# Quantised attention stage: values projected behind the queries, bias split and residual moved to other engines, one comparison per threshold, and a new order of every engine's instructions

## Time and profile before

| | before |
|---|---|
| median of 3 runs | 3001.84 us (2989.6 to 3002.13) |
| profiled execution, its own time | 3000.46 us |
| its span | 2998.6 us |
| PE busy | 2708.6 us (90%) |
| DVE busy | 1938.4 us (65%) |
| ACT busy | 1374.7 us (46%) |
| POOL busy | 1243.1 us (41%) |
| mean granted clock of TensorE | 0.934 of full speed |

### The profile page before, as it was taken

How to read it: one execution, slowest core, us unless ns; L and a number is a source line. 1 busy time by engine, 2 the same in 40 slices (tenths; PEclk the granted TensorE clock), 3 DMA queues, 4 the chain that set the end, 5 groups by cost and what they waited for, 6 DMA issues and landing times. The chain is left out here.

```text
span 2998.6 us, 65391 instructions
## 1 busy us (share of the span) xinstructions
PE 2708.6 (90%) x23572; PEld 2325.2 (78%) x23572; DVE 1938.4 (65%) x4184; ACT 1374.7 (46%) x3256; POOL 1243.1 (41%) x1637
## 2 busy tenths in 40 slices
PE   7999999978999999999997999867777888599995
PEld 7999999966888888888887788755666666477774
DVE  5565555556777777777775544357766666466666
ACT  3222222235666666666665333233333333266665
POOL 2111111125767767676774011223333434334434
PEclk9999999998999999999999999977777878799998
DMA  5000000001000000000000100000000000000001
GB/s 179 7 7 7 7 7 7 3 10 51 4 5 3 5 5 3 5 3 5 3 5 24 50 0 0 8 28 8 8 7 7 7 7 0 18 30 28 28 11 57
DMA packets 43501, 49.58 MB, mean 17 GB/s; under 512 B 4064, under 2 KB 33728, under 8 KB 43168
## 3 DMA queue, kind: packets, MB, share of 16 engines
q1 hardware_dynamic: 43424, 48.55, 4.9%
HBM read 35.96 MB, written 4.19 MB: 13 GB/s over the span
## 5 line engine op out<-in xcount | busy, mean ns | idle before, releaser
L587 POOL TENSOR_TENSOR a_probs<-a_probs,a_rs 128x512 f32<-128x512 f32 x64 | 70.7, 1104 | 466.7 <-DVE a_rs L443 466.7
L1108 ACT ACTIVATE b_probs<-bank,b_shift,b_q_scale 128x128 f32<-128x128 f32 x512 | 228.5, 461 | 0.6
L1173 POOL TENSOR_TENSOR b_rows<-b_rows,b_swapped 128x512 f32<-128x512 f32 x160 | 204.6, 1287 | 57.3 <-DVE b_swapped L946 57.3
L1220 POOL TENSOR_TENSOR b_probs<-b_probs,b_rs 128x512 f32<-128x512 f32 x128 | 133.4, 1042 | 137.8 <-DVE b_rs L998 134.7
L531 ACT COPY a_pT<-bank 128x512 f32<-128x512 f32 x64 | 37.6, 587 | 308.7 <-PE bank L324 308.7
L448 DVE TENSOR_TENSOR a_oT<-bank,a_oT 128x512 fp32r<-128x512 f32 x128 | 82.5, 687 | 144.1 <-ACT a_oT L536 144.1
L1183 POOL TENSOR_TENSOR b_rms<-b_rms,sh_minus_half 128x8 f32<-128x8 f32 (+1 forms) x128 | 170.6, 1333 | 10.7
L954 DVE TENSOR_REDUCE b_ss<-b_squares 128x4 f32<-128x512 f32 x192 | 125.3, 681 | 73.5 <-ACT b_squares L1083 73.5
L2728 ACT ACTIVATE d_probs<-d_probs,d_unit_q 128x512 f32<-128x512 f32 x128 | 90.5, 721 | 163.5 <-DVE d_probs L2612 163.0
L46 PE MATMUL bank<-a_xT,early_wq 128*128 128x256 f32 x512 | 150.4, 294 | 13.1 <-DVE early_wq L73 10.5
L46 PE MATMUL bank<-early_wo,b_oT 128*128 128x256 f32 x512 | 150.3, 293 | 1.4 <-DVE b_oT L920 1.4
(11 more groups left out here) (379 smaller groups left out, 9252.8 us busy)
## 6 DMA issues: line engine op xcount, KB each, us to landing
a_xT_in<-in_xT SPq DMA_DIRECT2D x16, 256.0 KB, 2.6
sh_x<-in_x SPq DMA_DIRECT2D x1, 4096.0 KB, 18.7
b_ctx_in<-in_ctxT SPq DMA_DIRECT2D x32, 128.0 KB, 2.0
d_x_in<-sh_x SPq DMA_DIRECT2D x16, 256.0 KB, 2.3
e_x_in<-sh_x SPq DMA_DIRECT2D x16, 256.0 KB, 2.3
e_cT<-in_ctxT SPq DMA_DIRECT2D x32, 128.0 KB, 2.5
out<-sh_x SPq DMA_DIRECT2D x16, 256.0 KB, 2.1
a_qT<-in_L_attn_Wq SPq DMA_DIRECT2D x4, 512.0 KB, 6.3
```

What stands on the lines that cost most here:

```text
L1108: op = act.activation(probs[:, g % 2, keys], bS[:, keys], ACT.Exp, bias=shift[:, g % 2, a:a + 1], scale=q_scale[:, g, a // 2, a % 2:a % 2 ...
L1173: pool.tensor_tensor(rows[:, unit, :], rows[:, unit, :], swapped[:, half, :], ALU.add).then_inc(added[unit], 1)
L1220: pool.tensor_tensor(pr, pr, rs[:, g % 2, :].unsqueeze(2).to_broadcast([128, R, 128]), ALU.mult).then_inc(probs_ready[g], 1)
```

```diff
-            def project_columns(bank, m, o):
+            def project_columns(i, bank, m, o, ready):
...
                 for c in range(C):
-                    exact(out, parts(lambda a: wq[:, m, a, c, o * 128:(o + 1) * 128]), (qx.result[:, c, :], qx.result[:, c, :]), c == 0)
-                return pe.matmul(out, qx.y_both[:, o * 128:(o + 1) * 128], of_chunk[:, m, :], start=False, stop=True)
+                    for a in range(2):
+                        pe.matmul(out, wq[:, m, a, c, columns], qx.result[:, c, :], start=(c == 0 and a == 0), stop=False)
+                pe.matmul(out, qx.y_high[:, columns], of_chunk[:, m, :], start=False, stop=False)
+                pe.matmul(out, qx.y_low[:, columns], of_chunk[:, m, :], start=False, stop=True).then_inc(ready, 1)
...
                 for c in range(C):
-                    op = pe.matmul(bank[0:q.reps, c * 128:(c + 1) * 128], q.cmax[:, c, :, :].rearrange("p k m -> p (k m)"),
-                                   sh.ident[:, :], start=True, stop=True)
+                    for j in range(len(weights)):
+                        pe.matmul(bank[32 * j:32 * j + 32, c * 128:(c + 1) * 128], q.cmax[:, c, :, :].rearrange("p k m -> p (k m)"),
+                                  sh.ident[:, :], start=True, stop=True)
...
-            def both_y(i, q, used):
...
-                dve.scalar_tensor_tensor(q.y_both[:, :], q.y_high[:, :].bitcast(F32), keep_low[0:q.reps, :], q.y_whole[:, :],
-                                         ALU.mult, ALU.add).then_inc(q.y_both_ready, 1)
...
+            def exceed(i, q):
...
+                dve.tensor_tensor(q.exceeds[:, :, :, :], q.cmax[:, :, 0, :].unsqueeze(3).to_broadcast([128, C, M, N_THR]),
+                                  q.thr[:, :, :].unsqueeze(1).to_broadcast([128, C, M, N_THR]), ALU.is_gt).then_inc(q.is_above, 1)
...
-                dve.tensor_tensor(q.by_column(q.clipped[:, :]), q.by_column(q.steps[:, :]), q.of_top(LEAST), ALU.max).then_inc(q.raw_scale, 1)
+                dve.scalar_tensor_tensor(q.by_column(q.clipped[:, :]), q.of_top(INVERSE), 1e-9, q.by_column(q.steps[:, :]),
+                                         ALU.mult, ALU.max).then_inc(q.raw_scale, 1)
+
+            def rescale(i, q):
...
+                dve.tensor_tensor(q.by_column(q.scale[:, :]), q.by_column(q.clipped[:, :]), q.of_top(UNIT), ALU.mult).then_inc(q.scale_ready, 1)
...
-                for r in range(2):
-                    op = dve.scalar_tensor_tensor(sh.res[:, r, :], bX[0][:, r * D:(r + 1) * D], unit_c[:, r:r + 1], xb[:, r, :], ALU.mult, ALU.add)
-                op.then_inc(res_ready, 1)
...
+            def take_y(i, r):
...
+                act.wait_ge(y_ready, this(i))
+                act.wait_ge(qc.unit_rows_ready, this(i))
+                act.wait_ge(res_ready, last(i))
+                op = act.activation(y_scaled[:, r, :], bX[0][:, r * D:(r + 1) * D], ACT.Copy, scale=unit_c[:, r:r + 1])
+                if r == 1:
+                    op.then_inc(scaled, 1)
...
-                pool.wait_ge(q.compared, nth(i.n, 2, 1))
-                hold(pool, sh.passed_pool)
-                pool.tensor_scalar(above, above, 0.0, None, ALU.is_gt).then_inc(q.compared, 1)
...
+            def low_y(i, q, used):
...
+                pool.tensor_tensor(q.y_low[:, :], q.y_whole[:, :], q.y_high[:, :].bitcast(F32), ALU.subtract).then_inc(q.y_low_ready, 1)
...
+            def residual(i):
...
+                pool.wait_ge(scaled, this(i))
+                pool.wait_ge(xb_ready, this(i))
+                pool.wait_ge(norm_done, last(i))
+                hold(pool, sh.passed_pool)
+                pool.tensor_tensor(sh.res[:, :, :], y_scaled[:, :, :], xb[:, :, :], ALU.add).then_inc(res_ready, 1)
```

```diff
+                exponent(new, 0)
+                exponent(new, 1)
+                take_y(old, 0)
+                take_y(old, 1)
+                take_pT(new, 0)
```

415 lines of the change are left out of this document (203 added, 212 removed).

## The result

| | before | with the change |
|---|---|---|
| median of 4 runs each | 3001.32 us (2989.6 to 3002.13) | 2832.16 us (2824.01 to 2835.54) |
| profiled execution, its own time | 3000.46 us | 2824.01 us |
| its span | 2998.6 us | 2822.2 us |
| mean granted clock of TensorE | 0.934 | 0.973 |

The ratio is 0.9441 (0.9409 to 0.9473): 5.6% faster. A difference of 0.3 us between the mean turns of two kernels is therefore not clear of noise; turns that are wholly at full clock agree in both profiles (27.3 to 27.5).

A forecast was written before the change was run, and what follows sets the result against it. It took a chain through one bank, with no engine full, to bound the quantised stage. Fourteen turns falling from 38.8 to 29.5 us give 130, with 12 at fill and drain 142: 3000.5 - 142 = 2858 us, range 2825 to 2915.

The forecast's parts named there:

- four parts (maxima, K, old rows, output): Old quantised turn of 38.8 us: x's chain, old rows' chain, output and residual follow each other through one bank.
- the wait in it for GpSimd: Old rows' divide and restore take 2.35 and 2.26 us during GpSimd's key spread, against 0.69 for x's restore.
- the walk through the new turn: New turn followed from x's turning at full clock: K's copy at 15.1, next x at 28.5, plus 1.0.
- fill and drain: First slots, last two turns and tail around the fourteen full turns: together 12 us less.
- TensorE's floor: Rival: TensorE's 25.2 us of work sets the turn, hand-offs hidden, 26 to 28 a turn, 2809 to 2837 us; chance 0.08.
- hand-offs: End of the new turn: 1.0 us added for waits between engines and one likely half-rate stretch, giving 29.5.
- Contention: Old rows' divide and restore beside GpSimd's key spread: 3.2 us of the chain lost in the turn shown.
- the five: Savings from x's maxima to K's copy: comparison 1.1, y_both 0.5, old maxima earlier 2.0, clock 0.8, multiplication 0.2; 4.6 in all.
- Half rate for two fifths of the time: Rival: TensorE's clock stays at 0.80 in the turns, 34 us a turn, 2921 us; chance 0.22.
- Keys late: Rival: a turn is K's copy plus 13.7; with K's copy at 29.3, 43.0 a turn, 3047 us; chance 0.06.

The follow-up runs named there:

- out of the way: Changed kernel with GpSimd's residual first, both low_y together, VectorE's shift and moments ahead of clip and rescale: 2823.15 us, ratio 0.9415.
- three passes: Changed kernel with GpSimd's three-pass comparison in place of VectorE's comparison and GpSimd's multiplication: 2874.29 us, ratio 0.9585.
- residual on VectorE: Changed kernel with the residual on VectorE again, last in its list, without ScalarE's scaled copies and GpSimd's sum: 2865.01 us, ratio 0.9551.
- fewer matmuls: Changed kernel without the eight matmuls that add the low part of the bias products: 2840.14 us, ratio 0.9473.
- the run: Changed kernel with the copy of K behind the restore of the old rows in VectorE's list: 2956.37 us, ratio 0.9883.

## Why the prediction was right, and where it was off

**What was right.** The chain of the old kernel with its four parts (maxima, K, old rows, output), the wait for GpSimd in it, and the points of the walk through the new turn, within 0.7 us up to the output. A clock above 0.9 was forecast too.

**The sum.** Predicted were turns of 29.5, 12 us at fill and drain, 2858 us. Against the profiled execution the miss is 34 us: 13 x (29.5 - 27.5) = 27 in the turns, 2.4 at the fill (5.4 for 3.0) and 5 behind (23.3 for 18.5). The median lies 8 us above that execution, hence 26. The turn of 27.5 and 2832 us are not in the likeliest band (28 to 31.5, chance 0.61) but in that of the rival *TensorE's floor*, whose words were "the hand-offs are hidden, 26 to 28 a turn, 2809 to 2837", with a chance of 0.08. The range held the result only because it took in half of that rival. The way and the direction were right; that the number came out inside is in part luck.

**The step that was off** is the last of the walk: "27.6 to 28.6, later with the hand-offs between ... I take 28.5 and add 1.0 for hand-offs". The next x was turned at 27.4 in the turn shown. The walk itself held, point by point (predicted, measured from 2081.79): x's maxima 4.1, 4.3; K's copy 15.1, 15.2; keys spread 20.0, 19.7; clip 18.1, 17.9; rescale 20.2, 19.8; old rows restored 23.6 to 24.6, 22.95; output 25.7, 26.3 (the terms given for the output, 20.0 + 2.1 + 0.6 + 1.2 + 1.5, make 25.4). After the restore its words "Then two maxima and two shifts 2.4, the exponent 0.721, two scaled copies of the output 0.9" were wrong: the copies start as the output is done and stand behind no exponent. The wait of "up to 1.0 behind GpSimd's normalisation" did not come (it was GpSimd that waited, see the end), and the half-rate stretch that the +1.0 partly stood for is in two of thirteen turns only. From K's copy to the next x the prediction had 28.5 - 15.1 = 13.4 and 1.0 for hand-offs, and it was 12.1 to 12.2. No row stood for the hand-offs; most of them must lie inside the rows' distances already, so they were counted twice.

**The bound was named wrongly.** "VectorE ... leaves 23. It is then no bound, only its order is." The 23 is what VectorE's work is: 26.4 busy less 3.6 of waiting is 22.8. The prediction had the rescale wait behind the keys in its walk (2.1 us predicted, 1.8 measured) and left it out of VectorE's list; the restore of x behind `low_y` and residual, 1.6 us, it did not see at all. With both, VectorE is busy for 26.4 of 27.5. The second wait is the one that matters: TensorE's hole of 1.4 us a turn stands behind it, and when 1.15 us of the wait and nearly all of the hole went (out of the way), a turn at full clock fell from 27.4 to 25.9. The first is not on the chain: the prediction held that without the rescale's wait a turn would be 26.5 and not 28.5, but with it nearly gone the way from K's copy to the next x stayed at 12.1. It hardly moved the number because it was offset: the unseen wait lies between x's maxima and K's copy, and that length still came out at 10.9 for 11.0, so the savings priced there must have been taken too small by as much. That is luck. The error would have misled whoever chose the next step.

**Contention** of 3.2 us a turn: right, and shown alone. Its worth in the old order was 5.0, with the clock's rise in it.

**Single prices:** `exceed` 0.275 (0.3), `rescale` 0.173 where nothing is beside it (0.2), `low_y` 0.75 (0.65), residual on GpSimd 1.29 (1.27), GpSimd in all 196.87 / 13 = 15.1 (15.5), maxima of x into column groups 0.46 and 0.86 from start to start against 0.60 and 1.00: 0.3 less, where 0.1 more was taken. TensorE is busy for 25.6 us in a turn at full clock (floor 25.2), by the busy time of one stretch of the changed kernel:

```profile
2110.16:2137.66 27.50, 25.59 (x331) 19.86 (x327) 26.62 (x58) 15.80 (x33) 15.49 (x26) 1.00 0.03 10
```

**The gain by part.** The prediction took 1.1 off K's way for the comparison, with no condition. The runs show that a gain was there only in the new order (nothing in the old, 42 us in the new, where K's copy moved by 1.8 us, at another clock). From the maxima of x to K's copy it had 11.0 and it was 10.9, but with 1.6 us of waiting in it that no term had; the sum agrees, its terms don't, and only this one of the five was tried alone.

**The rivals.** Half rate for two fifths of the time: no, clock 0.99. It stays as a thing near by: three passes, residual on VectorE, and even fewer matmuls bring stretches of it back. TensorE's floor: the turn lies in this rival's band, 27.5 for a work of 25.6, and what keeps it from the floor is the hole at x's restore; the last order, with 25.9 at full clock, is at the floor. Keys late: its form holds, a later copy makes a longer turn, but its 13.7 was 12.1 in the changed kernel, and the 13.8 of the run stands for a lower clock. The copy there, at 20.5, is short of the 25 from which the prediction had it slower than before, and the kernel was still 1.2% faster than before.

**Engines that shut each other out.** The restore of x and the rescale each take 1.6 us more where GpSimd works beside them than where it does not. The Trainium skill (SBUF — State Buffer, Who interferes with whom) has the two exclude each other for whole instructions; the trace agrees, down to an instruction of 16 columns (1818 against 173 ns). In the walk I had applied it to the keys, and not to the two `low_y` and the residual.

## What to carry to other kernels

Walk a strict-order kernel's turn as a chain, and then look, in the trace of the result, for the holes of the engine with the most work: they name the wait that is on the chain. A busy share does not; here VectorE showed 26.4 us a turn for 22.8 of work, and of its two large waits the one at the restore of x cost the turn 1.4 us and the one at the rescale nothing. A wait behind another engine's instruction is not removed by moving the instruction: it jumps to whatever two-input operation is then there, unless one that reads a bank, or none, is put beside the busy neighbour. A part's worth belongs to an order: the same comparison was worth 0 us in the old one and 42 in the new, so measure parts by taking them out of the new kernel as well as by putting them into the old.
